# LSTM stage of a four-layer graph kernel: one written order per engine for a whole turn, the two groups merged freely

## What is computed

```python
h = relu(layernorm(x))
h = relu(einsum('ts,bsh->bth', adj, h @ Wg0 + bg0))
h = relu(einsum('ts,bsh->bth', adj, h @ Wg1 + bg1))
for p in range(1, 5):                       # windows of p rows
    nw = 128 // p
    wins = h[:, :nw * p].reshape(B * nw, p, 128)
    # one LSTM over the p rows of a window, state starts at zero
    #   i, f, g, o = split(x_t @ Wih[p-1].T + h @ Whh[p-1].T + bias)
    #   c = sigmoid(f) * c + sigmoid(i) * tanh(g);  h = sigmoid(o) * tanh(c)
    last = lstm_last(Wih[p-1], Whh[p-1], bih[p-1], bhh[p-1], wins)
    h = h.at[:, arange(nw) * p + p - 1].set(last)
x = x + h
```

## Time and profile before

| what | value |
|---|---|
| median of 3 runs | 1310.18 us (1309.94 to 1312.72) |
| profiled execution, its own time | 1309.45 us |
| its span, first to last instruction | 1307.6 us |
| TensorE matmuls, busy | 1192.5 us, 91% |
| VectorE, busy | 1010.0 us, 77% |
| ScalarE, busy | 812.9 us, 62% |
| POOL, busy | 412.6 us, 32% |
| TensorE's mean granted clock, of full speed | 0.979 |

### The profile page before, as it was taken

The page is one execution under the profiler, slowest core; times in us unless marked ns, Lnnn a source line. Parts: engine busy times, 40 slices in busy tenths (PEclk is TensorE's granted clock), DMA queues, the critical chain, the costliest instruction groups (busy, mean ns, idle before and its releaser), DMA issues. The chain is left out here.

```text
span 1307.6 us, 24530 instructions
## 1 busy us (share of the span) xinstructions
PE 1192.5 (91%) x7808; PEld 1024.9 (78%) x7808; DVE 1010.0 (77%) x2796; ACT 812.9 (62%) x1804; POOL 412.6 (32%) x779
## 2 busy tenths in 40 slices
PE   2889999899899998998999799998999899968998
PEld 1678788787787886877878688886777688857997
DVE  6677877878778778777787699997777578775776
ACT  3477575775765757757667576776777376742332
POOL 3110200200102002001020277775767488832332
PEclk7899999999999999999999899999999899988999
DMA  9300000000000000000000000000000000001222
GB/s 269 93 1 1 1 1 1 0 0 0 0 0 0 0 0 0 0 0 0 0 1 1 1 2 2 2 2 1 1 1 1 1 1 2 2 1 40 72 72 72
DMA packets 24728, 21.09 MB, mean 16 GB/s; under 512 B 1744, under 2 KB 20304, under 8 KB 24400
## 3 DMA queue, kind: packets, MB, share of 16 engines
q1 hardware_dynamic: 24656, 20.21, 5.4%
HBM read 11.82 MB, written 8.39 MB: 15 GB/s over the span
## 5 line engine op out<-in xcount | busy, mean ns | idle before, releaser
L557 ACT ACTIVATE gate<-ps,b_lstm 128x256 f32<-128x256 f32 (+2 forms) x624 | 300.4, 558 | 36.8 <-PE ps L584 36.8
L582 PE MATMUL ps<-H_hi,w_hi 128*128 128x256 f32 (+2 forms) x624 | 212.4, 342 | 42.1 <-ACT gate L557 25.3
L583 PE MATMUL ps<-H_hi,w_lo 128*128 128x256 f32 (+2 forms) x624 | 205.3, 330 | 0.0
L584 PE MATMUL ps<-H_lo,w_hi 128*128 128x256 f32 (+2 forms) x624 | 195.9, 335 | 6.6 <-DVE H_lo L526 5.2
L126 POOL TENSOR_SCALAR rstd<-mv 128x8 f32<-128x8 f32 x18 | 12.3, 685 | 600.5 <-DVE mv L107 600.4
L582 PEld LDWEIGHTS ps<-H_hi,w_hi 128*128 128x128 f32 x624 | 117.5, 188 | 68.2 <-ACT gate L557 32.6
L567 ACT ACTIVATE tanh_c<-cell 128x512 f32<-128x512 f32 (+2 forms) x176 | 90.4, 514 | 127.6 <-DVE cell L517 81.7
L584 PEld LDWEIGHTS ps<-H_lo,w_hi 128*128 128x128 f32 x624 | 114.6, 189 | 25.1 <-DVE H_lo L526 17.5
L583 PEld LDWEIGHTS ps<-H_hi,w_lo 128*128 128x128 f32 x624 | 117.8, 189 | 7.6
L582 PE MATMUL ps<-hid_hi,w_hi 128*128 128x256 f32 (+2 forms) x384 | 119.0, 316 | 0.8 <-DVE hid_hi L523 0.8
L583 PE MATMUL ps<-hid_hi,w_lo 128*128 128x256 f32 (+2 forms) x384 | 117.3, 312 | 0.0
(11 more groups left out here) (206 smaller groups left out, 3102.8 us busy)
## 6 DMA issues: line engine op xcount, KB each, us to landing
out<-x SPq DMA_DIRECT2D x32, 256.0 KB, 2.3
w_raw<-in_WihT SPq DMA_DIRECT2D x1, 1024.0 KB, 8.6
w_raw<-in_WhhT SPq DMA_DIRECT2D x1, 1024.0 KB, 8.1
wqkvT<-in_WqkvT SPq DMA_DIRECT2D x1, 192.0 KB, 4.9
w_sb<-in_W SPq DMA_DIRECT2D x1, 192.0 KB, 4.6
ends_row<-in_src_row SPq DMA_DIRECT2D x1, 128.0 KB, 3.6
ends_row<-in_dst_row SPq DMA_DIRECT2D x1, 128.0 KB, 3.7
x<-in_x_in SPq DMA_DIRECT2D x8, 0.5 KB, 10.5
```

Source lines behind the costliest of these rows:

```text
L557: nc.scalar.activation(gate[:, g, z, 0:w * GB], gate_bank(g, k, m)[:, 0:w * GB], ACT.Tanh if z == G else ACT.Sigmoid, bias=b_lstm[:, 4 * ( ...
L582: nc.tensor.matmul(dst, w_hi[:, src, p - 1, z], v_hi, start=start, stop=False)
L583: return nc.tensor.matmul(dst, w_lo[:, src, p - 1, z], v_hi, start=False, stop=False)
L584: return nc.tensor.matmul(dst, w_hi[:, src, p - 1, z], v_lo, start=False, stop=stop)
```

## The change

The two groups are no longer one item apart. For each of TensorE, VectorE and ScalarE the work of a group's turn is cut into parts in a fixed sequence, and a string of letters says whose part comes next: a and b for the groups, s and t for the next turn's normalisation of a and b; a capital letter is a part that belongs to the turn before. The parts are smaller than the items were: TensorE's input share is apart for each gate (SHARE), a step is HIGH (high terms of two gates), LOW (their low terms) and REST for each further gate; VectorE's step is KEEP, CELL, HIDDEN and LOW; ScalarE's is one GATE each and TANH. Graph layers go by chunk. The matmuls, products and activations themselves, their shapes and their operands stay. ScalarE gets a wait on the cell of step 0 before two gates of step 1, and one on A0's matmuls before the first normalised row; POOL's two calls of a turn are written in one place.

```diff
@@ -392,35 +391,59 @@
-        A0, OUT, W0, U1, A1, STEP = range(6)
-        ITEMS = STEP + NS
-
-        STATS_AT = {U1: (0, 3), A1: (3, 3), STEP: (6, 2)}
-        AGGR_AT = STEP + 1
-        APPLY_AT = {STEP + 3: (0, 1), STEP + 4: (1, 2), STEP + 5: (3, 2), STEP + 6: (5, 1), STEP + 8: (6, 1),
-                    STEP + 9: (7, 1)}
-
...
+        A0, OUT, W0, U1, A1, SHARE, HIGH, LOW, REST, GATE, KEEP, CELL, TANH, HIDDEN, STATS, AGGR, APPLY = range(17)
+
+        def recurrent(k):
+            return steps[k][1] > 0
+
+        by_chunk = lambda *what: [(q, c, 0) for q in what for c in range(CH)]
+        TENSOR_PARTS = by_chunk(A0, OUT, W0, U1, A1)
+        VECTOR_PARTS = by_chunk(OUT, W0, U1, A1)
+        SCALAR_PARTS = by_chunk(A0, A1)
+        for k in range(NS):
+            n = len(gates_of[k])
+            TENSOR_PARTS += [(SHARE, k, m) for m in range(n) if recurrent(k)] + [(HIGH, k, 0), (LOW, k, 0)]
+            TENSOR_PARTS += [(REST, k, m) for m in range(2, n)]
+            VECTOR_PARTS += [(KEEP, k, 0)] * recurrent(k) + [(CELL, k, 0), (HIDDEN, k, 0)] + [(LOW, k, 0)] * (k < NS - 1)
+            SCALAR_PARTS += [(GATE, k, m) for m in range(n)] + [(TANH, k, 0)]
+        MOMENTS = [(STATS, j, 0) for j in range(GB)] + [(AGGR, 0, 0)]
+        NORMED = [(APPLY, j, 0) for j in range(GB)]
+
+
+        ON_TENSOR = ("BBBaaaaBBBaBBbabbababaabbaababbaaabbbbbaaaaaabaaaabbbbabbbbbbaaaabaaaaaaaabbaaabbaaabbabbbbababb"
+                     "bababbbbaaaaaaaaabbbbbaabbaaaabbaaabbbabbabaaabbbb")
+        ON_VECTOR = ("saassstaBBBastssbtsbaastbaatbbttbaabbaaabatbbabaabbaabbbaabbataabbaabaabbaaaabbabbaabbbbaabaabba"
+                     "aabbabbaabbabb")
+        ON_SCALAR = ("aaBBBBBbbaaaaaabbaaaabbbsbbaabaabbsaaabbbbsaabbbsaaaasbbaaaatbbabbsaaaaabbbtbaabttaabbbbbaaaasbb"
+                     "abbtstaaaaabbbbtbaaabbbbaatb")
+
+        def merged(engine, order, do, main, side):
+
+            parts = {"a": main, "b": main, "s": side, "t": side}
+            late = {z: order.count(z.upper()) for z in parts}
 
             def turn(i, first, last):
-                for n in range(ITEMS):
-                    for do, g, behind in parts:
-                        if n >= behind:
-                            do(i, g, n - behind, not last, not first)
-                        elif not first:
-                            do(i - 1, g, n - behind + ITEMS, True, True)
+                taken = {z: len(parts[z]) - late[z] for z in parts}
+                for letter in order:
+                    z = letter.lower()
+                    part = parts[z][taken[z] % len(parts[z])]
+                    taken[z] += 1
+                    g = int(z in "bt")
+                    if last and i == TURNS:
+                        if letter != z:
+                            do(TURNS - 1, g, *part, True)
+                        elif part[0] == OUT:
+                            do(TURNS, g, *part, True)
+                    elif letter == z:
+                        do(i, g, *part, not first)
+                    elif not first:
+                        do(i - 1, g, *part, True)
...
+            turn(TURNS - 1, False, False)
+            turn(TURNS, False, True)
...
-                def item(i, g, n, more, _):
-                    if n == AGGR_AT:
+                def turn(i):
+                    for g in range(2):
                         make_rstd(pool, i + 1, g)
 
-                interleave(pool, [(item, 0, 0), (item, 1, 1)])
+                turn(0)
+                with pool.Fori(1, TURNS - 1) as i:
+                    turn(i)
+                turn(TURNS - 1)
...
-                        if j == 0:
+                        h32, h_hi, h_lo = hidden(k, g)
+                        tc = flat(tanh_c[:, g], w)
+                        if what == KEEP:
+                            dve.wait_ge(sa(g, "a_gate"), n0 + 2)
+                            nc.vector.tensor_tensor(gi, gi, gg, ALU.mult).then_inc(sa(g, "a_part"), 1)
+                        elif what == CELL and j == 0:
+                            dve.wait_ge(sa(g, "a_gate"), n0 + 2)
                             nc.vector.tensor_tensor(cc, gi, gg, ALU.mult).then_inc(sa(g, "a_cell"), 1)
-                        else:
-                            nc.vector.tensor_tensor(gi, gi, gg, ALU.mult).then_inc(sa(g, "a_part"), 1)
+                        elif what == CELL:
                             dve.wait_ge(sa(g, "a_gate"), n0 + 3)
                             nc.vector.tensor_tensor(cc, cc, gf, ALU.mult).then_inc(sa(g, "a_part"), 1)
                             dve.wait_ge(sa(g, "a_part"), i * TP + parts_before[k] + 2)
                             nc.vector.tensor_tensor(cc, cc, gi, ALU.add).then_inc(sa(g, "a_cell"), 1)
-                        norm_piece(i + 1, g, n)
-                        h32, h_hi, h_lo = hidden(k, g)
-                        tc = flat(tanh_c[:, g], w)
-                        dve.wait_ge(sa(g, "a_tanh"), i * NS + k + 1)
-                        if k < NS - 1:
+                        elif what == HIDDEN and k < NS - 1:
+                            dve.wait_ge(sa(g, "a_tanh"), i * NS + k + 1)
                             nc.vector.tensor_tensor(h_hi, go, tc, ALU.mult).then_inc(sa(g, "a_hid"), 1)
                             nc.vector.tensor_tensor(h32, go, tc, ALU.mult).then_inc(sa(g, "a_h32"), 1)
+                        elif what == HIDDEN:
+                            dve.wait_ge(sa(g, "a_tanh"), i * NS + k + 1)
+                            nc.vector.tensor_tensor(h32, go, tc, ALU.mult).then_inc(sa(g, "a_hid"), 1)
+                        elif what == LOW:
                             dve.wait_ge(sa(g, "a_h32"), i * (NS - 1) + k + 1)
                             nc.vector.tensor_tensor(h_lo, h32, h_hi.bitcast(F32), ALU.subtract).then_inc(
                                 sa(g, "a_lo"), 1)
-                        else:
-                            nc.vector.tensor_tensor(h32, go, tc, ALU.mult).then_inc(sa(g, "a_hid"), 1)
-
-                interleave(dve, [(item, 0, 0), (item, 1, 1)])
+
+                merged(dve, ON_VECTOR, part, VECTOR_PARTS, MOMENTS)
...
+                        z = gates_of[k][m]
+                        act.wait_ge(sa(g, "a_gatep"), i * TG + gates_before[k] + m + 1)
+                        if apart[k] and z == O:
+                            act.wait_ge(sa(g, "a_h32"), i * (NS - 1) + k)
+                        elif apart[k]:
+                            act.wait_ge(sa(g, "a_cell"), i * NS + k)
+                        nc.scalar.activation(gate[:, g, z, 0:w * GB], gate_bank(g, k, m)[:, 0:w * GB],
+                                             ACT.Tanh if z == G else ACT.Sigmoid,
+                                             bias=b_lstm[:, 4 * (p - 1) + z:4 * (p - 1) + z + 1]).then_inc(
+                                                 sa(g, "a_gate"), 1)
+                    elif what == TANH:
                         w = steps[k][4]
                         act.wait_ge(sa(g, "a_cell"), i * NS + k + 1)
                         nc.scalar.activation(tanh_c[:, g, 0:w * GB], cell[:, g, 0:w * GB],
                                              ACT.Tanh).then_inc(sa(g, "a_tanh"), 1)
-                        if n in APPLY_AT:
-                            relu_norm(act, i + 1, g, *APPLY_AT[n])
-
-                interleave(act, [(item, 0, 0), (gates, 0, 0), (cell_tanh, 0, 0),
-                                 (item, 1, 1), (gates, 1, 1), (cell_tanh, 1, 1)])
+                    elif what == APPLY:
+                        if k == 0:
+                            act.wait_ge(sa(g, "a_shift"), i + 2)
+                            act.wait_ge(sa(g, "a_axp"), i * CH + CH)
+                        relu_norm(act, i + 1, g, k, 1)
+
+                merged(act, ON_SCALAR, part, SCALAR_PARTS, NORMED)
...
+                    elif what == SHARE:
+                        p, j, last, w0, w = steps[k]
+                        pe.wait_ge(sa(g, "a_gate"), i * TG + gates_before[k] + m - 3)
+                        for half in (0, 1):
+                            term(g, k, m, 0, at(H_hi[:, g], p, j, w0, w), at(H_lo[:, g], p, j, w0, w), True, False, half)
                     else:
-                        step(i, g, n - STEP)
-
-                interleave(pe, [(input_share, 0, 0), (input_share, 1, 1), (item, 0, 0), (item, 1, 1)])
+                        p, j, last, w0, w = steps[k]
+                        src = int(j > 0)
+                        v = ((hid_hi[:, g, 0:w * GB], hid_lo[:, g, 0:w * GB]) if j else
+                             (at(H_hi[:, g], p, j, w0, w), at(H_lo[:, g], p, j, w0, w)))
+                        if what == HIGH:
+                            if k == 0:
+                                pe.wait_ge(sa(g, "a_Hlo"), i * CH + CH)
+                            elif not apart[k]:
+                                pe.wait_ge(sa(g, "a_hid"), i * NS + k)
+                            for q in (0, 1):
+                                if apart[k] and gates_before[k] + q >= 4:
```

(52 more changed lines are left out.)

184 lines of the change are left out of this document (65 added, 119 removed).

## The result

| | median us | runs |
|---|---|---|
| before | 1311.33 (1309.94 to 1312.72) | 4 |
| after | 1249.80 (1249.16 to 1250.47) | 4 |
| ratio | 0.9531, 95% interval 0.9514 to 0.9547 | |

The kernel is 4.7% faster; 1252.6 was forecast. The profiled execution took 1249.93 us with a span of 1248.2. Busy time by stretch in the profile after: the LSTM stage, what follows it, and one turn of the loop, measured between two like matmuls.

What follows compares the result with a forecast made beforehand. TensorE was nearest to full, waiting about 9 us of each 86.7 us LSTM turn. 77.6 work plus 1.9 waits gave 79.5, saving 57.6 us over eight turns: 1251.9 profiled, 1252.6 us median, range 1237 to 1285.

Steps and rivals of the forecast that it cites:

- TensorE's floor: LSTM loop: TensorE's necessary work, taken as 77.6 us of each 86.7 us turn, unchanged by the edit.
- the two counts: TensorE's work per turn, from spacing of matmul starts (76.8 us) and from turn time less gaps (78.2 us).
- 1.9 us of waits stay: TensorE waiting left per turn under the new order, estimated at 0 to 3 us, taken as 1.9.
- six tight places: Hand-overs to TensorE at the head, a 2, a 5, b 3, a 7, b 7: 0 to 0.5 us lost each.
- Only order moves time: LSTM loop: compute instructions and shapes stay, added waits and POOL's power are hidden, so only waits can move.
- 0.5 us for a part that asks at once: VectorE: price of each HIDDEN directly behind its group's cell update, from twelve hid_hi waits costing 6.5 us.
- The hand-over counts: TensorE's other matmuls covering a group's chain between LOW and next HIGH; none of 18 hand-overs counted short in new order.
- 2 of the 9 us: TensorE's old waiting per turn: about 2 of 9 us visible as short covers, the rest from helper queues.
- A: Rival: ScalarE's and VectorE's queues keep half of the 9 us waiting; 82 to 83.5 us a turn, chance 0.25.
- B: Rival: all covers hold and TensorE reaches its floor; 76.8 to 78.2 us a turn, 1231 to 1242 us, chance 0.1.
- C: Rival: no change, because gaps come from the four banks of a group rather than from order; chance 0.05.
- D: Rival: the three lists block each other; a loss from 0.5 us per hand-over, 1345 us at 0.75; chance 0.1.

Runs made afterwards that it cites:

- experiment 7: Changed kernel, but A0's two chunks wait for 37 and 38 gates of the group's turn instead of all 39: 1243.00 us, ratio 0.949.
- experiment 1: Changed kernel with all three order strings spelling the order of before; finer parts and new waits stay: 1309.76 us, ratio 1.000.
- experiment 4: Changed kernel, in VectorE's order CELL, HIDDEN and LOW stand together in 20 of 22 steps: 1306.44 us, ratio 0.998.
- experiment 5: Changed kernel, in ScalarE's order TANH directly behind its own step's gates in 22 places instead of 16: 1289.88 us, ratio 0.984.
- experiment 10: Changed kernel with all old orders, TensorE's recurrent matmuls reading constant weights instead of hidden states, waits added on ScalarE: 1317.23 us.
- experiment 2: Changed kernel with TensorE's list in the order of before, VectorE's and ScalarE's lists new: 1372.46 us, ratio 1.047.
- experiment 3: Changed kernel, in VectorE's order HIDDEN directly behind its group's CELL in 20 of 22 places instead of 7, LOW unmoved: 1355.38 us, ratio 1.037.
- experiment 12: Experiment 1's kernel, in VectorE's list b's HIDDEN and LOW of steps 0 to 8 moved behind a's next CELL: 1465.45 us, ratio 1.116.

## Why the prediction was right, point by point

- **TensorE's floor, 77.6 us a turn.** Right: 79.30 less its 1.65 of waits is 77.65, and 78.11 less the 0.58 left in experiment 7 (0.98 by the same count, less the 0.40 that is no wait) is 77.5, both between the 76.8 and 78.2 of the two counts. The formula of the Trainium skill (TensorE: Matmul & The Clock Gate, Back-to-back issue gap), which the page gives for an isolated matmul, would have put the floor 5 us lower, and the about 131 ns that the same section gives for 512 columns in a stream with weight loads lower still; the trace after agrees with the rows instead, 0.23 us from 216.55 over 216.78 and 217.02 to 217.25 at 512 columns.
- **1.9 us of waits stay.** Near in size (1.65; 2.0 by the prediction's count), wrong in most of its places. b's step 0 lost 0.40 - 0.23 = 0.17 against the 0.2 worked out, and a's step 5, one of the six tight places, 0.40. b's step 1, put at 0.5, has no gap of 0.15 or more. The largest, 1.1 us at the two A0, was not among the tight places at all: I counted what a part needs, and not what its wait asks for, and A0 asks for all gates. That part of the sum was right by luck.
- **Only order moves time.** Right: experiment 1 shows it under the old order. That POOL's power and the new waits cost nothing under the new one is read from the trace after, where every wait of a gate ends on TensorE and no normalised row of the turn waits.
- **0.5 us for a part that asks at once.** Right for VectorE: 0.55 by experiment 4. For ScalarE nothing was priced; experiment 5 gives 0.8.
- **The hand-over counts.** The covers nearly hold under the new order (0.95 us a turn). As the account of the old one they were only part of it. The prediction said that 2 of the 9 us showed as short covers and the rest came from queues; experiment 10 (old orders without the recurrence) says that the old turn, at the full clock, doesn't move when the hand-overs to TensorE are taken away. Counting covers told which new order would do, and not what bound the old one.
- **The rivals.** A, the queues giving half back (82 to 83.5 us a turn), didn't come; B, the floor (76.8 to 78.2), was missed by 1.1, and experiment 7 reaches its upper end with 78.11. C fell with experiment 1 and the result. D, lists that hold each other up, didn't happen here, but is real: experiments 2, 3 and 12 are 63, 46 and 154 us slower than before, through waits of this kind and the lower clock that came with them. Its threshold, 0.5 us at 18 hand-overs, is close to what one early part costs; its chance of 0.1 rested on the covers.

Open: what set the old turn, beyond that it was not TensorE's waits for hidden states; whether any list of VectorE or ScalarE alone could have sped up the old order; and whether the last 0.58 us of waits could be closed.

## What to carry to other kernels

Where engines run fixed lists, price the order of all of them as one thing: two good lists beside an old third lost 63 us here, and taking away TensorE's waits for hidden states didn't shorten the old turn. Give each list something of another stream between producing a value's input and asking for the value (0.55 to 0.8 us per place here), but never behind a wait that comes later than the consumer needs. And once an order is tight, look at what each wait asks for: a wait for two gates too many was free before and cost 7 us after.

## What the hardware showed unasked

TensorE's granted clock fell in the kernels with long waits. Busy time by stretch in experiment 12, first where TensorE waited, then soon after (PEclk is the third number from the end):

```profile
412.00:414.70 2.70, 0.63 (x5) 0.35 (x3) 2.07 (x5) 2.02 (x6) 0.00 (x0) 1.00 0.00 0
...
416.70:419.30 2.60, 2.60 (x11) 2.60 (x10) 1.16 (x3) 2.41 (x6) 0.00 (x0) 0.50 0.00 0
```

And experiment 2, the matmuls behind a wait, with a stretch of the same view below:

```profile
271.57 0.42 PE L598 MATMUL ps<-H_hi,w_hi 128*128 128x336 f32 x1 [1.67 <-DVE H_hi L541]
...
274.02 0.63 PE L598 MATMUL ps<-hid_hi,w_hi 128*128 128x512 f32 x1
274.44 0.63 PE L599 MATMUL ps<-hid_hi,w_lo 128*128 128x512 f32 x1
```

```profile
274.00:276.50 2.50, 2.50 (x7) 2.01 (x7) 0.00 (x0) 0.11 (x1) 0.00 (x0) 0.50 0.00 0
```

Some 2 us behind idle times of 2.1 and 1.7 us (0.4 more in between) the clock is at its lower level, 1.2 GHz, for these 2.5 us, and in experiment 2 the 512-wide matmuls start 0.42 us apart instead of 0.23. Over the turn it was 0.96 in experiment 2 and 0.93 in experiment 12. The single waits of before, up to 1.43 us, had left it at 1.00. The length of a wait does not decide it alone. In experiment 10 the same wait for a bank comes in every turn, and in one turn the clock stays up behind 2.63 us of it (252.70 us), in the next it falls behind 2.60 (339.33 us):

```profile
253.50:256.00 2.50, 2.50 (x15) 2.24 (x14) 1.80 (x4) 1.05 (x3) 0.00 (x0) 1.00 0.00 0
340.10:342.60 2.50, 2.50 (x8) 1.92 (x7) 1.80 (x4) 0.96 (x2) 0.00 (x0) 0.50 0.00 0
```

These two turns take 86.66 and 88.11 us. So a long stall can cost more than its length: here 1.45 us, and in experiments 2 and 12 TensorE's busy time in the turn is 85.1 and 88.1 us instead of 80.5. The pricing of rival D had no term for that.
